# Whole weighted sum ahead of the query, attention output turned ahead of the next scores: the tile loop of a gated cross-attention and expert block

## The chip, the cores and the metric

One core of a Trainium2 chip. The time is device microseconds of one execution; the kernel before was run three times, and one further execution was profiled. All times below are microseconds (us) from the start of the profiled span unless said otherwise. PE is TensorE (PEld its weight loads), DVE is VectorE, ACT is ScalarE, POOL is GpSimd, SP is SyncE.

## The reference

```python
# x (2, 1024, 256), context (2, 77, 256), 16 heads of 16
x = x + tanh(g_xattn) * cross_attention(layernorm(x), ctx)   # scores, mask, softmax, probs @ V, @ wo.T + bo
# 8 experts, top 1
def ffn(xt):
    gates, idx = max and argmax of softmax(xt @ Wr + br)
    xn = layernorm(xt) * ln_g + ln_b
    h = relu(xn @ W1[idx] + b1[idx])
    return (h @ W2[idx] + b2[idx]) * gates
x = x + tanh(g_ffn) * ffn(layernorm(x))
```

## The kernel before, in words

The 2048 tokens are 16 tiles of 128 (`NT = 16`, `TPB = 8` a batch). The first half of the kernel is a loop `for n in range(NT)` over tiles, written out by hand for each engine; the engines meet only through semaphores, and each works through its own list in order. The second half routes the tokens, sorted by expert, through slots of 128 rows; it begins when the loop is done.

The tile loop is a pipeline. In round n, PE does the scores of tile n, `transpose_O(n-2)` (the normed attention output `On` is turned into `pA`), `transpose_P(n-1, 0)` (the first probabilities are turned into `pT`), `project(n-2)` (the turned output `OT` times `wo`, into `pB`), `transpose_P(n-1, 1)`, `transpose_x(n+1)`, `transpose_P(n-1, 2)`, the weighted sum `attend(n-1)` (probabilities times values, into `pB`, ten chunks) with its first 8 chunks, `query(n+1)`, the other 2 chunks, and `route(n)` (the router's product, moving width 8). In round 13 (`NT - 3`) PE also does `ranks(0)`, ahead of `route`; it waits for the one-hot rows `oh` of tiles 0 to 10.

DVE in round n: max and subtraction of the first half of the scores (L923, L931), with the two steps of `gate(n-4)` between them in rounds 4 to 12 (L1010, L1016); `resid(n-2)` (L957: adds `pB` to `xs`, after `project(n-2)`; `attend(n-1)` may only then write `pB`); the second half's max and subtraction; statistics (L962, L966, L891, L895); the steps of `router(n-3)`, a generator (L990, L994, L999, L1003 which makes `oh`, L1005); `normed1(n+2)` (L901, makes xh); then `norm(n-1)`, a generator of three steps (L940 waits for the weighted sum, L944, L950 makes `On`), with router steps between them; `logits` and `x_logits`. Round 3 has three steps of `mask_bias(1)`. From round 14 on, steps of a table (`table_steps`) fill in between; `rank(0)` is one of its two generators and makes 11 rows of a table (L1090).

ACT copies or activates what PE turned: `copy_OT` (L639), `copy_PT` (L629 to L633), `exp` (L621), `copy_XX` (L602), `query` (L615), and writes the z and x2 parts of the row that POOL stores to DRAM (`z_row` L657, `x2_row` L650), and `gate_exp` (L662). SP's loads of the last three experts' weights wait for counts of `x2_row`. POOL has the powers of the norms, `x + bias`, and the stores of the rows.

`pA` is shared by `transpose_O`, `transpose_x` and the first half of the query; `pB` by the weighted sum, the projection and, later, the outputs of the experts. The waits that matter here are these:

```python
def transpose_O(i):
    e.wait_ge(g["dve_On"], i + 1)
    e.wait_ge(g["act_Q"], 2 * min(i + 2, NT - 1) + 1)
def project(i):
    e.wait_ge(g["act_OT"], i + 1)
# attend, at chunk 0
    e.wait_ge(g["dve_x2"], i)
# ranks
    e.wait_ge(g["dve_oh"], hi)
```

Of the kernel before, what the change touches and what calls it, by code (L numbers as in the profile page):

```python
# [20 lines left out]
NT = T // 128  # L21
# [10 lines left out]
NC = 10  # L32
# [36 lines left out]
def flamingo(nc, x, ctx_in, mask, g_x, g_f, wq, bq, wk, bk, wv, bv, wo, bo,  # L69
# [5 lines left out]
    with ExitStack() as ctx:  # L75
# [135 lines left out]
        g = {n: sem(n) for n in EVENTS}  # L211
# [383 lines left out]
        def _(e):  # L595
# [87 lines left out]
            for n in range(NT):  # L683
                if n >= 2:
                    copy_OT(n - 2)
                if n:
                    copy_PT(n - 1, 0)
                exp(n, 0)
                if n == 0:
                    exp(0, 1)  # L690
                if n:
                    copy_PT(n - 1, 1)
                    if n + 1 < NT:
                        copy_XX(n + 1)
                    copy_PT(n - 1, 2)
                    exp(n, 1)
                if n == 1:
                    e.wait_ge(g["pe_wT"], 4)
                    e.wait_ge(g["act_tg"], 1)
                    e.activation(wT["wo"][:, :, 0:D], bank["T1"].rearrange("p (k d) -> p k d", k=2), ACT.Copy,  # L700
                                 scale=tg[:, 0:1]).then_inc(g["act_wT"], 1)
                if n + 1 < NT:
                    query(n + 1)
                if n >= 3:
                    z_row(n - 3)
                if n == 2:
                    e.wait_ge(g["dve_pois"], 1)
                if n >= 2:
                    x2_row(n - 2)
                if n >= 3:  # L710
                    gate_exp(n - 3)
                if n == 1:
                    e.wait_ge(g["pe_wT"], 5)
                    e.wait_ge(g["pe_lg"], 2)
                    e.activation(wT["wo"][:, :, D:DX], bank["T1"][:, 0:16].rearrange("p (k d) -> p k d", k=2),
                                 ACT.Copy, scale=tg[:, 0:1]).then_inc(g["act_wT"], 1)
                    e.activation(boR[:, :], bank["T1"][:, 16:24], ACT.Copy, scale=tg[:, 0:1]).then_inc(g["act_wT"], 1)
            r_of = {}

# [165 lines left out]
        def _(e):  # L885
# [351 lines left out]
            def table_steps(k):  # L1237
                for _ in range(k):
                    next(tabled, None)

            for n in range(NT):
# [5 lines left out]
                t = smax(n, 0)  # L1247
# [25 lines left out]
                if n == 3:  # L1273
                    e.wait_ge(g["dve_pois"], 1)
                    mask_bias(1)
                next(routed, None)
                next(x_stats, None)
                table_steps(3)
                next(routed, None)
                if n + 2 < NT:  # L1280
                    normed1(n + 2)
# [292 lines left out]
        def _(e):  # L1574
# [84 lines left out]

            def attend(i, chunks=range(NC)):  # L1660
                b = i // TPB
                if i == 0:
                    e.wait_ge(g["dve_VB"], 2)
                for c in chunks:
                    n = chunk_rows(c)
# [3 lines left out]
                    if c == 0 and i:  # L1669
                        e.wait_ge(g["dve_x2"], i)  # L1670
                    t = e.matmul(pB[:, 17 * h0:17 * h0 + 51], PT[i % 2][0:n, c, :], VB[0:n, b, c, :], start=(c == 0),  # L1671
                                 stop=(c == NC - 1), skip_group_check=True)
                if c == NC - 1:
                    t.then_inc(g["pe_PV"], 1)

# [84 lines left out]
            for n in range(NT):  # L1760
                scores(n)
                if n >= 2:
                    transpose_O(n - 2)
                    transpose_P(n - 1, 0)
                    project(n - 2)
# [30 lines left out]
                if n:  # L1796
# [7 lines left out]
                    transpose_P(n - 1, 2)  # L1804
                    attend(n - 1, range(8 if n > 1 else NC))
                if n == 1:
                    e.wait_ge(g["act_PT"], 2)
                    weight("wo", "T1")
                if n + 1 < NT:
                    if n >= 1:  # L1810
                        e.wait_ge(g["act_PT"], 3 * n)
                    query(n + 1)
                if n > 1:
                    attend(n - 1, range(8, NC))
                if n == 0:
# [23 lines left out]
                if n:  # L1839
                    route(n)  # L1840

            def first_ids():
# [268 lines left out]
```

## Time and profile before

| what | value |
|---|---|
| median of 3 runs | 278.11 us (276.93 to 278.54) |
| profiled execution | 278.49 us, its span 276.7 us |
| PE busy | 268.3 us, 97% of the span |
| PEld busy | 238.7 us, 86% |
| DVE busy | 201.5 us, 73% |
| ACT busy | 166.3 us, 60% |
| POOL busy | 131.9 us, 48% |
| chain that ended last | PE 80%, DVE 8%, issue 6% |
| mean granted TensorE clock | 0.991 |

Busy time says how long an engine had something to do. The end of a matmul is modelled, so a PE that is reported busy can still have waited a little; the weight loads (PEld) show idle time more plainly, and the time from one group of instructions to the next shows what a round really costs.

### The profile page before, as it was taken

The page shows a single profiled execution, that of the slowest core. Times are in us where ns is not written, and L with a number is a line of the kernel's source. Part 1 is how long each engine was busy: PE and PEld are TensorE (multiplying, and loading weights), DVE is VectorE, ACT ScalarE, POOL GpSimd, SP SyncE. Part 2 cuts the span into 40 slices and gives each one's busy share as a digit, 9 for nine tenths or more (in the row PEclk, how much of TensorE's full clock was granted, in tenths as well). Part 3 has the DMA queues.
Part 4 walks back from the last instruction along what each step waited for, and adds up shares of the span by engine and source line. Part 5 has one row for each costly group of instructions (what it writes and reads, how often), then busy time and mean ns, then how long its engine had stood idle before and what let it go on. Part 6 is the DMA issues. An engine that isn't in the chain of part 4 may idle for free.

```text
span 276.7 us, 7230 instructions
## 1 busy us (share of the span) xinstructions
PE 268.3 (97%) x2310; PEld 238.7 (86%) x2310; DVE 201.5 (73%) x687; ACT 166.3 (60%) x444; POOL 131.9 (48%) x255
## 2 busy tenths in 40 slices
PE   8999999999999999999999999999999999999993
PEld 4879899999899999988899799899878799988992
DVE  6699479888888888899679966985547545543564
ACT  2435467777677777676776655795438445453551
POOL 3444146677877778644775424432322042222421
PEclk9999799999999999999999999999999999999998
DMA  7999998010112464565343131412201122120222
GB/s 213 257 307 374 372 376 286 5 38 39 41 40 52 191 191 186 189 195 190 116 118 118 48 104 48 129 50 80 60 23 46 49 63 61 61 57 27 59 60 61
DMA packets 19948, 34.42 MB, mean 124 GB/s; under 512 B 2392, under 2 KB 14486, under 8 KB 19899
## 3 DMA queue, kind: packets, MB, share of 16 engines
q1 hardware_dynamic: 15945, 22.33, 24.8%
q0 software_dynamic: 3808, 11.42, 13.3%
q8 instruction: 25, 0.41, 0.6%
q14 instruction: 24, 0.20, 0.2%
q10 hardware_dynamic: 146, 0.07, 0.1%
HBM read 27.45 MB, written 6.75 MB: 124 GB/s over the span
## 4 chain that ended last, share of the span: by engine, by line
PE 80%; DVE 8%; issue 6%; POOL 3%; DMA 2%; DVEq 0%; POOLq 0%
PE pS L1897 17%; PE pB L1671 12%; PE pB L1967 9%; PE pT L1582 7%; PE pB L1689 7%; PE pA L1582 5%; PE pB L1972 4%; PE pS L1625 4%; PE pA L1605 3%; PE pT L1605 2%; PE pT L1699 2%; POOL out_dram L473 1%; POOL zin L456 1%; DMA W2s<-in_ctx_dram 1%; DVE hA L1346 1%
## 5 line engine op out<-in xcount | busy, mean ns | idle before, releaser
L1897 PE MATMUL pS<-znf,W1c 128*128 128x128 f32 x576 | 71.0, 276 | 0.3 <-DVE ticks L1334 0.3
L1897 PEld LDWEIGHTS pS<-znf,W1c 128*128 128x128 f32 x576 | 67.2, 192 | 3.0 <-issue 2.9
L473 POOL DMA_INDIRECT out_dram<-yo,idxs x17 | 17.2, 1010 | 76.4 <-DVE yo L1377 72.4
L1967 PE MATMUL pB<-W2p,hT 128*128 128x512 f32 x136 | 38.9, 408 | 0.5 <-DVE ticks L1386 0.4
L761 ACT ACTIVATE hA<-pS,b1s 128x128 f32<-128x128 f32 x72 | 20.5, 367 | 30.5 <-PE pS L1897 24.9
L1346 DVE TENSOR_SCALAR hA<-pS,b1s 128x128 f32<-128x128 f32 x72 | 20.2, 344 | 20.3 <-PE pS L1897 19.9
L621 ACT ACTIVATE Pb<-Pb 128x616 f32<-128x616 f32 x32 | 23.0, 718 | 15.4 <-DVE Pb L931 15.4
L772 ACT ACTIVATE hT<-hA 128x512 fp32r<-128x512 f32 x36 | 22.9, 640 | 14.5 <-DVE hA L1346 14.5
L1967 PEld LDWEIGHTS pB<-W2p,hT 128*128 128x128 f32 x136 | 23.0, 188 | 5.9 <-issue 2.1
L923 DVE TENSOR_REDUCE mx<-pS 128x8 f32<-128x616 f32 x32 | 25.3, 789 | 1.8 <-PE pS L1629 1.8
L456 POOL DMA_INDIRECT zin<-rows_dram,idxg x21 | 22.1, 1051 | 9.5 <-issue 5.3
L931 DVE TENSOR_TENSOR Pb<-pS,mx 128x616 f32<-128x616 f32 x32 | 25.3, 792 | 0.8
L1582 PE MATMUL pT<-cst,Pb 128*128 128x128 f32 (+1 forms) x160 | 25.5, 277 | 0.0
L1353 DVE TENSOR_TENSOR hT<-hA,hT 128x512 fp32r<-128x512 f32 x36 | 24.3, 687 | 1.4 <-ACT hT L772 0.2
L1972 PEld LDWEIGHTS pB<-W2p,hT 128*128 128x128 f32 x136 | 20.7, 188 | 3.3 <-DVE hT L1353 0.3
L1972 PE MATMUL pB<-W2p,hT 128*128 128x256 f32 x136 | 21.6, 280 | 0.0
L1582 PEld LDWEIGHTS pT<-cst,Pb 128*128 128x128 f32 (+1 forms) x160 | 19.5, 142 | 2.1 <-issue 0.2
L1689 PE MATMUL pB<-woT,OT 128*128 128x264 f32 x64 | 19.2, 425 | 0.5
L1671 PE MATMUL pB<-VB,PT 128*128 128x51 f32 (+1 forms) x160 | 19.5, 270 | 0.0
L1671 PE MATMUL pB<-VB,PT_xh 128*128 128x51 f32 (+1 forms) x160 | 19.4, 270 | 0.0
L1671 PEld LDWEIGHTS pB<-VB,PT 128*128 128x128 f32 (+1 forms) x160 | 19.0, 192 | 0.3 <-issue 0.2
L1671 PEld LDWEIGHTS pB<-VB,PT_xh 128*128 128x128 f32 (+1 forms) x160 | 19.0, 192 | 0.3 <-issue 0.3
(282 smaller groups left out, 546.6 us busy)
## 6 DMA issues: line engine op xcount, KB each, us to landing
W1s<-in_L_ffn_W_dram SPq DMA_DIRECT2D x8, 1024.0 KB, 10.8
W2s<-in_L_ffn_W_dram SPq DMA_DIRECT2D x8, 1024.0 KB, 11.4
rows_dram<-pay POOLq DMA_DIRECT2D x12, 260.0 KB, 3.9
xs<-in_x_dram SPq DMA_DIRECT2D x3, 512.0 KB, 8.6
rows_dram<-pay SPq DMA_DIRECT2D x4, 260.0 KB, 2.0
W2s<-in_sel_dram SPq DMA_DIRECT2D x1, 385.0 KB
zin<-rows_dram,idxg POOLq DMA_INDIRECT x21, 3.7
out_dram<-yo,idxs POOLq DMA_INDIRECT x17
```

The source lines that it names most:

```text
L456: e.indirect_dma_start(zin[s % NZ][:, :], None, scratch[0:128 * GA, :] if s < KA else scratch, bass.IndirectOffsetOnAxis(ap=idxg[:, s:s + ...
L621: e.activation(p2, p2, ACT.Exp, scale=0.25).then_inc(g["act_P"], 1)
L923: e.tensor_reduce(mx[:, i % 2, 8 * m:8 * m + 8].rearrange("p (n h) -> p n h", n=2), heads(m), AX.X, ALU.max).then_inc(g["dve_own"], 1)
L931: e.tensor_tensor(Pb[i % 2][:, 616 * m:616 * m + 616].rearrange("p (n h k) -> p n h k", n=2, h=4), heads(m), mx[:, i % 2, 8 * m:8 * m + 8] ...
L1346: e.tensor_scalar(half_of(s, 1)[:, 128 * c:128 * c + 128], pS[:, 2 * (s % 2) + 1, 128 * c:128 * c + 128], b1s[:, 4 + c, s:s + 1], 0.0, ALU ...
L1353: e.tensor_tensor(lo, half_of(s, n)[:, :], hi, ALU.subtract).then_inc(g["dve_hT"], 1)
L1582: return e.transpose(o, i, ident[0:n, 0:n])
L1671: t = e.matmul(pB[:, 17 * h0:17 * h0 + 51], PT[i % 2][0:n, c, :], VB[0:n, b, c, :], start=(c == 0), stop=(c == NC - 1), skip_group_check=True)
L1689: t = e.matmul(pB[:, 0:DX], OT[:, k, :], wT["wo"][:, k, :], start=(k == 0), stop=(k == 1))
L1897: t = e.matmul(pS[:, 2 * (s % 2) + n, 128 * c:128 * c + 128], W1c[k][n][:, 128 * c:128 * c + 128], znf[s % 2][:, 128 * k:128 * k + 128], s ...
L1967: e.matmul(o2, hT[s % 2][0][:, 128 * c:128 * c + 128], W2p[c // 2][:, :, D * (c % 2):D * (c % 2) + D], start=False, stop=True, skip_group_ ...
L1972: t = e.matmul(o, hT[s % 2][1][:, 128 * c:128 * c + 128], W2p[c // 2][:, 0, D * (c % 2):D * (c % 2) + D], start=False, stop=True, skip_gro ...
```

## The change

It moves work within the tile rounds; no instruction is added or dropped. PE does all ten chunks of `attend(n-1)` ahead of `query(n+1)`, and turns the output of tile n-1 at the end of round n (rounds 1 to 14) where it turned that of tile n-2 behind the scores. ACT copies the turned output behind the query's copies, and the z row is written ahead of the second `exp`. DVE takes the three steps of the norm earlier (not in round 15): the first ahead of the aggregate of the x statistics, the others between the router's first steps; `normed1` and the rest of the router's steps come behind it.

```diff
--- before.py
+++ after.py
@@ -681,8 +681,6 @@
             copy_XX(1)
             a_steps = Count()
             for n in range(NT):
-                if n >= 2:
-                    copy_OT(n - 2)
                 if n:
                     copy_PT(n - 1, 0)
                 exp(n, 0)
@@ -693,6 +691,8 @@
                     if n + 1 < NT:
                         copy_XX(n + 1)
                     copy_PT(n - 1, 2)
+                    if n >= 3:
+                        z_row(n - 3)
                     exp(n, 1)
                 if n == 1:
                     e.wait_ge(g["pe_wT"], 4)
@@ -701,8 +701,8 @@
                                  scale=tg[:, 0:1]).then_inc(g["act_wT"], 1)
                 if n + 1 < NT:
                     query(n + 1)
-                if n >= 3:
-                    z_row(n - 3)
+                if 2 <= n < NT - 1:
+                    copy_OT(n - 1)
                 if n == 2:
                     e.wait_ge(g["dve_pois"], 1)
                 if n >= 2:
@@ -715,6 +715,7 @@
                     e.activation(wT["wo"][:, :, D:DX], bank["T1"][:, 0:16].rearrange("p (k d) -> p k d", k=2),
                                  ACT.Copy, scale=tg[:, 0:1]).then_inc(g["act_wT"], 1)
                     e.activation(boR[:, :], bank["T1"][:, 16:24], ACT.Copy, scale=tg[:, 0:1]).then_inc(g["act_wT"], 1)
+                    copy_OT(0)
             r_of = {}
 
             def regs(s):
@@ -1274,9 +1275,15 @@
                     e.wait_ge(g["dve_pois"], 1)
                     mask_bias(1)
                 next(routed, None)
+                if n < NT - 1:
+                    next(normal, None)
                 next(x_stats, None)
+                if n < NT - 1:
+                    next(normal, None)
                 table_steps(3)
                 next(routed, None)
+                if n < NT - 1:
+                    next(normal, None)
                 if n + 2 < NT:
                     normed1(n + 2)
                 table_steps(3)
@@ -1657,11 +1664,11 @@
                                   Pb[i % 2][:, 128 * c:128 * c + n])
                 t.then_inc(g["pe_PT"], 1)
 
-            def attend(i, chunks=range(NC)):
+            def attend(i):
                 b = i // TPB
                 if i == 0:
                     e.wait_ge(g["dve_VB"], 2)
-                for c in chunks:
+                for c in range(NC):
                     n = chunk_rows(c)
                     h0 = chunk_head(c)
                     if c % 4 == 0:
@@ -1670,8 +1677,7 @@
                         e.wait_ge(g["dve_x2"], i)
                     t = e.matmul(pB[:, 17 * h0:17 * h0 + 51], PT[i % 2][0:n, c, :], VB[0:n, b, c, :], start=(c == 0),
                                  stop=(c == NC - 1), skip_group_check=True)
-                if c == NC - 1:
-                    t.then_inc(g["pe_PV"], 1)
+                t.then_inc(g["pe_PV"], 1)
 
             def transpose_O(i):
                 e.wait_ge(g["dve_On"], i + 1)
@@ -1760,7 +1766,6 @@
             for n in range(NT):
                 scores(n)
                 if n >= 2:
-                    transpose_O(n - 2)
                     transpose_P(n - 1, 0)
                     project(n - 2)
                 if n == 1:
@@ -1802,7 +1807,7 @@
                     if n + 1 < NT:
                         transpose_x(n + 1)
                     transpose_P(n - 1, 2)
-                    attend(n - 1, range(8 if n > 1 else NC))
+                    attend(n - 1)
                 if n == 1:
                     e.wait_ge(g["act_PT"], 2)
                     weight("wo", "T1")
@@ -1810,8 +1815,6 @@
                     if n >= 1:
                         e.wait_ge(g["act_PT"], 3 * n)
                     query(n + 1)
-                if n > 1:
-                    attend(n - 1, range(8, NC))
                 if n == 0:
                     e.wait_ge(d["ln"], 48)
                     e.wait_ge(g["dve_V"], 2)
@@ -1838,6 +1841,8 @@
                     ranks(0)
                 if n:
                     route(n)
+                if 1 <= n < NT - 1:
+                    transpose_O(n - 1)
 
             def first_ids():
```

## Rows read from the trace of the kernel before

**Rows 1.** Stretches, score matmuls: stretch, us, busy (count), clock, DMA share, GB/s

```profile
28.99:37.40 8.41, 1.00 (x17) 0.80 1.07 380
...
87.55:94.65 7.10, 0.81 (x16) 1.00 0.55 186
...
108.84:116.55 7.71, 0.81 (x16) 1.00 0.53 173
```

**Rows 2.** Groups of lines, PEld, 44.49 to 108.84

```profile
L1689 PEld LDWEIGHTS pB<-woT,OT 128*128 128x128 f32 x36 | 6.1, 189 | 3.1 <-ACT OT L639 2.5
```

**Rows 3.** Timeline, PEld and PE, tile 10: start, us, engine, line, what

```profile
88.30 0.20 PEld L1582 LDWEIGHTS pA<-cst,On 128*128 128x128 f32 x2 [0.17 <-DVE On L950]
...
89.22 0.74 PEld L1689 LDWEIGHTS pB<-woT,OT 128*128 128x128 f32 x4 [0.28 <-ACT OT L639]
89.22 1.16 PE L1689 MATMUL pB<-woT,OT 128*128 128x264 f32 x4
...
90.98 1.86 PEld L1671 LDWEIGHTS pB<-VB,PT 128*128 128x128 f32 x16
92.76 0.53 PEld L1605 LDWEIGHTS pA<-XX,wqT 128*128 128x128 f32 x4
...
94.10 0.53 PEld L1699 LDWEIGHTS pT<-wrc,XX 128*128 128x128 f32 x4
```

**Rows 4.** Timeline, DVE, tile 10

```profile
88.46 0.78 DVE L923 TENSOR_REDUCE mx<-pS 128x8 f32<-128x616 f32 x1
89.17 0.15 DVE L1010 RECIPROCAL Lg<-Lg 128x1 f32<-128x1 f32 x1
...
90.07 0.20 DVE L1016 TENSOR_SCALAR pay<-Lg,tg 128x1 f32<-128x1 f32 x1
90.41 0.43 DVE L957 TENSOR_TENSOR xs<-pB,xs 128x264 f32<-128x264 f32 x1
...
94.35 0.17 DVE L940 TENSOR_SCALAR rden<-pB 128x16 f32<-128x16 f32 x1 [0.65 <-PE pB L1671]
...
94.92 0.43 DVE L950 TENSOR_TENSOR On<-pB,rden 128x256 f32<-128x256 f32 x1
```

**Rows 5.** Timeline, all engines, tile 8

```profile
73.61 0.72 PE L1629 MATMUL pS<-bias,identb 128*128 128x308 bf16 x4
...
74.37 0.80 DVE L923 TENSOR_REDUCE mx<-pS 128x8 f32<-128x616 f32 x1 [0.52 <-PE pS L1629]
```

**Rows 6.** Timeline, DVE and PEld, tile 13

```profile
114.19 0.41 DVE L901 TENSOR_SCALAR PT_xh<-xs,mv 128x256 f32<-128x256 f32 x1
114.51 0.15 DVE L999 TENSOR_REDUCE em<-Lg 128x1 f32<-128x8 f32 x1
114.70 0.23 DVE L1003 TENSOR_SCALAR oh<-cst,em 128x8 bf16<-128x8 f32 x1
...
115.33 0.44 PEld L1708 LDWEIGHTS pT<-oh,onesb 128*128 128x128 bf16 x11
...
116.01 0.52 PEld L1699 LDWEIGHTS pT<-wrc,XX 128*128 128x128 f32 x4
```

**Rows 7.** Timeline, DVE, tiles 14 and 15

```profile
117.44 0.79 DVE L923 TENSOR_REDUCE mx<-pS 128x8 f32<-128x616 f32 x1
...
119.49 0.43 DVE L957 TENSOR_TENSOR xs<-pB,xs 128x264 f32<-128x264 f32 x1
...
121.95 0.13 DVE L990 TENSOR_REDUCE Lg<-Lg 128x1 f32<-128x8 f32 x1
...
124.73 0.79 DVE L923 TENSOR_REDUCE mx<-pS 128x8 f32<-128x616 f32 x1
```

**Rows 8.** Timeline, PE, and a stretch with its granted clock (after POOL's count)

```profile
26.66 1.06 PE L1828 MATMUL pT<-wrc,W1s 128*128 128x8 f32 x8
...
30.00:31.00 1.00, 1.00 (x5) 1.00 (x6) 0.90 (x3) 0.35 (x1) 0.00 (x0) 0.50 1.08 401
```

**Rows 9.** Stretch of all engines: clock, DMA share and GB/s stand last

```profile
130.00:131.00 1.00, 0.99 (x16) 0.48 (x15) 0.95 (x8) 0.60 (x2) 0.90 (x3) 1.00 0.00 0
```

## The prediction

> **What bounds the kernel now.** I read the page first: PE is busy for 97% of the span and 80% of the chain that ended last. The stretches of the tile stage, taken on the score matmuls alone, give the rhythm: a tile of the loop costs 7.10 us from scores to scores, tile 2 costs 8.41 and tile 13 costs 7.71 [rows 1]. I call the start of a tile's scores S and give all times in a tile from S. Then the weight loads of nine tiles: the wait for `OT` (the copy of the turned output) ahead of `project` is 2.5 us in all, 0.28 a tile [rows 2]. The timeline of tile 10 (S = 87.55) places it: turning O starts at 0.75, `project` loads at 1.67 after 0.28 of idling, the weighted sum (`attend`) loads at 3.43, its first 16 records take 1.78 (0.111 each, so 0.22 for one turned output of two records), the query's load follows, and the last product starts at 6.55 with 0.55 until the next scores, 0.10 more than its four records need [rows 3]. The 0.17 of idling ahead of turning O is not a loss: in tile 8, where bias matmuls follow the scores, these too start 0.74 after S (72.87) and wait for nobody [rows 5].
>
> VectorE (DVE) is the second row to read. In tile 10 the max of the scores starts at 0.91, the second gate step at 2.52, the residual at 2.86, the moment `project` ends (1.67 + 1.16 = 2.83), and it ends at 3.29. `attend` may not write `pB` before that. DVE then idles 0.65 before the norm, which starts at 6.80 and has `On` ready 1.00 later [rows 3, 4].
>
> **What goes and what is added.** No instruction is added or dropped; turning O, the norm, the copy of O and the z row move.
>
> Part 1, the wait for `OT`. O of tile n-1 is now turned behind the last product of tile n, and the copy (0.15 to 0.55 after the next S, estimated from 0.38 us of copy) is done before `project` wants it at 1.17 (1.67 less 0.28 of wait, less 0.22 of turning). PE alone would then reach `attend` at 2.93 (3.43 - 0.28 - 0.22). If nothing else bound it, a tile would save the whole 0.28.
>
> Part 2, what is late next: the residual. The max starts at 0.85, because scores end at 0.81 and DVE, no longer carrying the norm there, follows PE by 0.04, as it does in tile 8 [rows 5]. From the max to the second gate step is 1.61 [rows 4]. The step itself lasts 0.20 and I give it 0.13, as DVE starts its next instruction some 0.07 before the end of the last. The residual starts at 0.85 + 1.61 + 0.13 = 2.59, ends at 3.02, and `attend` loads at 3.08. That is 0.35 earlier than 3.43, not 0.50. The 0.22 of turning O comes back at the end of the tile: 0.35 - 0.22 = 0.13, and I take 0.12. Bounds: 0.28 if `attend` doesn't wait for the residual, -0.07 if DVE doesn't overlap. The row decides between these: the max lasts 0.78 and the next starts 0.71 behind it [rows 4]. The Trainium skill, "VectorE: DVE Perf Modes", section "The DRAIN you can't avoid", says that the next instruction doesn't start until the pipe is empty. Read as full durations with no overlap, it would put the residual about 0.2 later and turn each tile's gain into that loss; the trace does not agree with that reading, by 0.07 us an instruction.
>
> Part 3, does turning O wait itself? `attend` loads at 3.08, 20 records take 2.22, the norm starts 0.25 behind the end (94.35 against 94.10 in tile 10; so 5.55), `On` is ready at 6.54. PE gets there at 5.30 + 0.90 (8 records of the query) + 0.45 (4 of the last product) = 6.65. Slack 0.1, so no wait, but no more than that. S of the next tile is 6.65 + 0.22 + 0.10 = 6.97. The query's copies on ScalarE are ready at the same moment within 0.05. The z row on ScalarE (0.5) fills the 0.58 of idling ahead of the second exp and costs nothing if that cover holds; if it doesn't, the query's copy still has 0.5 of slack. The copy of O goes ahead of the x row, which triggers the last weight loads; that delays them by some 0.4 to 0.9, and the DMA engines are already empty at 130.0, well before the routed stage needs the weights [rows 9].
>
> Tiles 4 to 7 and 9 to 12: 8 x 0.12 = 1.0 saved. Tile 8: the scores end 0.5 later and DVE is late by as much, so `attend` comes only 0.19 earlier and the 0.22 of turning is not covered: 0.0. Tile 3: three more small steps of DVE sit ahead of the norm now: 0.0. The entry (tiles 1, 2): the first O is turned before the clock falls, worth about 0.2, and one more turning lies ahead of tile 3: 0.0, bounds -0.25 and +0.25.
>
> Part 4, the price, in tile 13. `ranks(0)` stands behind the query in PE's order and waits for the one-hot row `oh` of tile 10, which DVE makes in this very tile. Before, DVE finished the router's steps without waiting for `attend`: `oh` is ready at 6.09 (114.70 + 0.22 - 108.84) and PE comes for it at 6.49 [rows 6]. Now the norm's first step stands in front of them in DVE's queue and waits for the whole weighted sum. This tile has no gate steps, so I put the residual 0.13 earlier, at 2.46; `attend` loads at 2.95 and ends at 5.17. The norm starts at 5.42 and `On` at 5.98 (0.57 behind, as in tile 10 [rows 4]); the next xh starts at 6.32 (0.1 ahead of the end of `On`), the min at 6.64 (0.32 behind), `oh` at 6.83 (0.19 behind) and is ready at 7.06 [rows 6]. PE has finished the query at 5.17 + 0.90 = 6.07 and waits until 7.12: a new stall of 1.05. Then the ranks, 0.68 [rows 6], the last product 0.45, turning O 0.22 and 0.10: the next S is at 8.57, against 7.71. Lost: 0.86. Bounds 0.6 and 1.0.
>
> Part 5, tiles 14 and 15. DVE works there without a break, from the max of tile 14 at 117.44 to that of tile 15 at 124.73, 7.29 [rows 7]. The norm's wait is put into that. The residual is at 2.05 behind the max as before (DVE's own pace), so `attend` loads at 0.85 + 2.05 + 0.49 = 3.39 and ends at 5.61; the norm can start at 5.86. DVE is there at 0.85 + (121.95 - 117.44) + 0.04 = 5.40. It idles 0.46, and 0.12 more between norm steps that the router's steps filled before. All of it is added to DVE's unbroken chain, so the max of tile 15 is 0.58 later; less 0.04 for its earlier start: 0.54 lost. From there (norm of tile 14, first ids, the tail) the order is unchanged and the delay is carried. Bounds 0.3 and 0.7.
>
> **The sum.** -1.0 (eight tiles) + 0.0 (tiles 1 to 3, 8) + 0.86 + 0.54 = +0.4 us. The profiled execution took 278.49 (span 276.7 and 1.8 around it); the median of the three runs is 0.4 lower, 278.11. On that median: 278.5. What a measurement of this kernel can tell from no change is about 0.5%, 1.4 us, so I forecast no change that can be told. With the bounds of all parts (-2.2 to +0.6 for the eight tiles, 0.6 to 1.0, 0.3 to 0.7, 0.25 either way) the forecast's own range is 276.5 to 280.6.
>
> **Rivals.**
> 1. *It does what it seems to do.* `attend` doesn't wait for the residual and PE saves 0.28 in each of some twelve tiles, and `oh` comes in time: 278.1 - 3.4 = 274.7. With the losses of parts 4 and 5 on top, 12 x 0.28 - 1.4 = 2.0, 276.1. For it: PE is the bound. Against: the residual's chain is DVE's own pace and reads 3.08 against 2.93. It decides if the residual ends before 2.87. Chance 0.13 for both.
> 2. *Slower: the clock.* In tile 2 PE is at its lower level (granted 0.50, so 1.2 of 2.4 GHz, from 30.0 to 31.0), soon after it did nothing but products of width 8 from 26.66 to the scores at 28.99 [rows 8], and the tile took 8.41 - 7.10 = 1.3 us more than the rhythm [rows 1]. In tile 13 PE would now idle 1.05 and then do narrow products for 1.1: 2.2 us of the same sort. If the clock falls there, 278.5 + 1.3 = 279.8. Against: half a microsecond of dense turning and scores follows at once, and before that comes a dense query. Chance 0.13. The Trainium skill, "TensorE: Matmul & The Clock Gate", Part 1, ties the level to how busy PE has lately been; the trace agrees that it fell behind thin work, and no run yet shows what idle time here does.
> 3. *Slower: turning O waits.* Part 3 has 0.1 of slack. If the norm comes 0.25 later than I reckon (the aggregate and the router step in between cost more than the steps that stood there), turning O waits 0.15 in nine tiles, +1.4: 279.9. Chance 0.12.
>
> **How the numbers follow.** Forecast 0.62, rivals 0.13, 0.13, 0.12. The two slow rivals lie at 279.8 and 279.9, just past the 279.5 that counts as slower; with a little of the forecast's upper end, slower gets 0.22. Faster needs 276.7: rival 1 and the forecast's lowest end, 0.15. No change 0.63. The range reaches to the slow rivals and to the milder form of rival 1: 276.2 to 280.2.
>
> **What the profile after would show.** From scores to scores 6.97 in the plain tiles, about 8.6 in tile 13, 7.5 in tile 14. PE's wait ahead of `project` gone, a short one ahead of `attend` on the residual, a wait of about 1 us at the ranks' first load on `oh`. DVE idle ahead of the norm 0.35 instead of 0.65. I am wrong if plain tiles read 6.82 (rival 1), if the granted clock falls below 1 behind tile 13 (rival 2), or if loads of the turned O idle on DVE's `On` (rival 3).

## The result, and the profile after

The changed kernel took 285.24 us (median of four executions: 281.71, 283.25, 287.22 and 289.06), the kernel before 277.88 beside it. The ratio is 1.018, with an interval of 1.011 to 1.025: slower, though the interval does not tell whether by 2%. The two longest of the four count as slow executions and are left out of the ratio. The forecast was 278.5, its range 276.2 to 280.2. The profiled execution took 281.71 (span 279.9, mean clock 0.985), the quickest of the four, so its profile shows only part of the loss.

First the windows from scores to scores, for tiles 10, 13 and 14; the columns are those of [rows 1].

```profile
87.13:94.23 7.10, 0.81 (x17) 1.00 0.48 186
108.42:117.58 9.16, 0.81 (x17) 1.00 0.45 145
117.58:126.23 8.65, 1.11 (x16) 0.80 0.45 156
```

The plain tile is as long as before, 7.10, and I had said 6.97. Tile 13 is 9.16 instead of 8.57, and tile 14, forecast at 7.5, is 8.65 at a mean clock of 0.80.

When the scores of tile 1 start differs from one execution to the next (18.46 before, 17.29 after; in all profiles 17.3 to 19.0), whatever the kernel. So I count from there to the end of the span; "rest" is tile 15 and all that follows the loop:

| from scores to scores | before | after | difference |
|---|---|---|---|
| tile 1 | 10.53 | 10.81 | +0.28 |
| tiles 2, 3 | 15.50 | 15.63 | +0.13 |
| tiles 4 to 12 | 64.35 | 64.69 | +0.34 |
| tile 13 | 7.71 | 9.16 | +1.45 |
| tile 14 | 7.15 | 8.65 | +1.50 |
| rest | 153.00 | 153.67 | +0.67 |
| sum | 258.24 | 262.61 | +4.37 |

The difference of the rest is no steady loss. In the five profiles of kernels with the changed end of the loop in which the clock did not fall there (this one and those of experiments 1, 2, 5 and 9), the rest lies between 152.9 and 154.4. In tiles 4 to 12 the loss stands in tile 4 (7.29, where the residual starts 0.19 later than in tile 10) and in tile 8 (7.72 against 7.59).

Where a plain tile's time went is read in the groups of PEld over the stretch of [rows 2], and then in the timeline of tile 10 (S = 87.13), the same tile as in [rows 3, 4].

```profile
L1695 PEld LDWEIGHTS pB<-woT,OT 128*128 128x128 f32 x36 | 6.1, 190 | 0.6
L1632 PEld LDWEIGHTS pS<-Kbd,QT 32*128 32x128 f32 x145 | 5.4, 184 | 1.7 <-ACT QT L615 1.5 <-issue 0.2
```

```profile
87.13 0.58 PEld L1632 LDWEIGHTS pS<-Kbd,QT 32*128 32x128 f32 x16 [0.17 <-ACT QT L615]
...
88.25 0.75 PEld L1695 LDWEIGHTS pB<-woT,OT 128*128 128x128 f32 x4
...
90.29 2.31 PEld L1678 LDWEIGHTS pB<-VB,PT 128*128 128x128 f32 x20 [0.26 <-issue]
92.51 0.53 PEld L1612 LDWEIGHTS pA<-XX,wqT 128*128 128x128 f32 x4
...
93.81 0.25 PEld L1589 LDWEIGHTS pA<-cst,On 128*128 128x128 f32 x2
94.23 0.44 PEld L1632 LDWEIGHTS pS<-Kbd,QT 32*128 32x128 f32 x12 [0.17 <-ACT QT L615]
```

DVE, and the second copy of the query on ACT, in the same tile:

```profile
88.00 0.80 DVE L924 TENSOR_REDUCE mx<-pS 128x8 f32<-128x616 f32 x1 [0.30 <-PE pS L1632]
...
89.75 0.42 DVE L958 TENSOR_TENSOR xs<-pB,xs 128x264 f32<-128x264 f32 x1
```

```profile
93.72 0.37 ACT L615 ACTIVATE QT<-pT,bcol 128x128 f32<-128x128 f32 x1
```

The wait for `OT` is gone, and turning O at 93.81 waits for nobody. `attend` now idles 0.26, and the residual (89.75 to 90.17) ended 0.12 before it. From `attend` to the next scores it is 3.94: 2.22 to the query, 0.90 to the last product (93.41), 0.40 to turning O and 0.42 from there to the scores. The last of these holds 0.17 of idling, which the view puts down to `QT`, the query's copy. But `QT` was ready at 94.09, 0.14 earlier. The same 0.17 stands behind the turned O where `QT` had been ready for longer: for 2.3 us ahead of the scores of tile 14, and for 0.33 ahead of those of tile 15:

```profile
125.86 0.20 PEld L1589 LDWEIGHTS pA<-cst,On 128*128 128x128 f32 x2
126.23 0.58 PEld L1632 LDWEIGHTS pS<-Kbd,QT 32*128 32x128 f32 x16 [0.17 <-issue]
```

So in the changed kernel PE's own order sets the scores once `attend` has begun, and the idling belongs to the step from turning O to the scores. Behind the last product, as the loop was before, it was 0.02. The one wait of the plain tile that could be taken out is that ahead of `attend`.

Tile 13, DVE, then PEld, then POOL, answers to [rows 6]:

```profile
113.92 0.18 DVE L941 TENSOR_SCALAR rden<-pB 128x16 f32<-128x16 f32 x1 [0.72 <-PE pB L1678]
...
114.49 0.42 DVE L951 TENSOR_TENSOR On<-pB,rden 128x256 f32<-128x256 f32 x1
...
115.34 0.75 DVE L1004 TENSOR_SCALAR oh<-cst,em 128x8 bf16<-128x8 f32 x1
```

```profile
116.16 0.35 PEld L1714 LDWEIGHTS pT<-oh,onesb 128*128 128x128 bf16 x11 [1.51 <-issue]
```

```profile
115.34 0.72 POOL L405 TENSOR_TENSOR xs<-xs,bob 128x256 f32<-128x256 f32 x1
```

The norm holds the router's steps back as foreseen, and the weight loads idle 1.51 ahead of the ranks. `oh` itself takes 0.75 where it took 0.23. It starts at the same moment as an instruction of POOL over 128x256 and ends 0.03 behind it. Behind this tile the clock falls, in these windows of all engines (granted clock third from the end):

```profile
117.00:118.00 1.00, 1.00 (x18) 0.83 (x21) 0.55 (x4) 0.32 (x2) 0.70 (x2) 0.97 0.00 0
118.00:119.00 1.00, 1.00 (x14) 0.69 (x11) 0.41 (x3) 0.65 (x4) 0.00 (x0) 0.50 0.46 179
```

It is 0.50, the lower level (1.2 of 2.4 GHz), for some 3.4 us. In the tile loop of the kernel before, the only such stretch was that of tile 2 [rows 8].

Tile 15 shows a wait that I had not reckoned with. The timelines of ACT and PEld:

```profile
133.95 0.51 ACT L650 ACTIVATE pay<-xs,pois 128x256 f32<-128x256 f32 x1 [1.63 <-DMA rows_dram<-pay]
...
134.56 0.36 ACT L639 ACTIVATE OT<-pA 128x256 f32<-128x256 f32 x1
```

```profile
129.95 2.31 PEld L1678 LDWEIGHTS pB<-VB,PT_xh 128*128 128x128 f32 x20 [1.04 <-issue]
...
134.97 0.74 PEld L1695 LDWEIGHTS pB<-woT,OT 128*128 128x128 f32 x4 [0.72 <-ACT OT L639]
```

And `attend(14)` on PEld in the kernel before:

```profile
127.33 2.31 PEld L1671 LDWEIGHTS pB<-VB,PT_xh 128*128 128x128 f32 x20 [0.27 <-issue]
```

The x2 row may only overwrite its staging buffer when an earlier row's store has left it. It waits 1.63 for that, and the copy of the turned output stands behind it in ACT's queue, with `project` behind the copy. The idling of 1.04 ahead of `attend(14)` looks dearer than it is: the sum loads 3.72 behind the tile's scores, where it loaded at 3.63 before with its waits spread over three places. It costs 0.1.

### The profile page after: what moved, and what is told of

It is laid out like the page before. It is cut to its first block, busy times and chain, and to the rows that moved or that the text cites. A ratio compares the mean times of both kernels' runs of the same rounds, so it can differ in the third digit from the quotient of the medians.

```text
span 279.9 us, 7230 instructions
## 1 busy us (share of the span) xinstructions
PE 268.6 (96%) x2310; PEld 237.2 (85%) x2310; DVE 202.9 (72%) x687; ACT 164.8 (59%) x444; POOL 132.9 (47%) x255
## 4 chain that ended last, share of the span: by engine, by line
PE 73%; DVE 9%; issue 8%; DMA 4%; POOL 4%; ACT 0%; DVEq 0%; POOLq 0%; ACTq 0%
PE pS L1902 17%; PE pB L1678 11%; PE pB L1972 9%; PE pT L1589 6%; PE pB L1695 5%; PE pB L1977 4%; PE pS L1632 4%; PE pA L1589 4%; PE pA L1612 3%; PE pT L1612 2%; DMA rows_dram<-pay 2%; PE pT L1705 2%; POOL out_dram L473 1%; DVE mx L924 1%; POOL zin L456 1%
## 5 line engine op out<-in xcount | busy, mean ns | idle before, releaser
L762 ACT ACTIVATE hA<-pS,b1s 128x128 f32<-128x128 f32 x72 | 20.5, 367 | 30.7 <-PE pS L1902 27.8
L1589 PE MATMUL pT<-cst,Pb 128*128 128x128 f32 (+1 forms) x160 | 27.0, 287 | 0.0
```

Source lines behind the costliest of these rows:

```text
L1589: return e.transpose(o, i, ident[0:n, 0:n])
```

## The experiments

Ratios are against the kernel before, run on the same chip beside them (its medians there 277.8 to 278.1). An edit is to the changed kernel unless it says otherwise.

### 1. The changed kernel again

No edit. The question was what the slower executions hold.

> The changed kernel itself, nothing edited, to see how far its executions lie apart and whether the granted clock goes with them (in four runs it took 281.7, 283.3, 287.2 and 289.1 us at mean clocks 0.985, 0.975, 0.968 and 0.957; before: 276.9 to 278.5, its profile at 0.991). Theory A (a clock that falls in the tile rounds, more often in some executions): times spread over 281 to 289 again, and every longer one has a lower clock, near 0.45 us for each 0.001. Theory B (waits alone, the spread is chance): the clock stays within 0.98 to 0.99 whatever the time.

Median 283.23 (281.32 to 287.00), ratio 1.018 (1.013 to 1.024). This time the profile fell on the slowest execution (287.00). Its windows of tiles 12 and 13:

```profile
101.21:112.28 11.07, 9.89 (x67) 0.75 0.35 124
112.28:123.52 11.24, 9.91 (x89) 0.79 0.40 118
```

Tiles 1 to 11 are as in the other profile within 0.05. What starts the loss is on the timelines of ACT, DVE and PEld in tile 12:

```profile
103.56 0.51 ACT L650 ACTIVATE pay<-xs,pois 128x256 f32<-128x256 f32 x1 [1.86 <-DMA rows_dram<-pay]
...
104.29 0.16 DVE L1011 RECIPROCAL Lg<-Lg 128x1 f32<-128x1 f32 x1 [1.40 <-ACT Lg L662]
...
104.79 0.18 PEld L1589 LDWEIGHTS pT<-cst,Pb 128*128 128x128 f32 x2 [0.87 <-ACT PT L629]
105.74 0.86 PEld L1678 LDWEIGHTS pB<-VB,PT 128*128 128x128 f32 x7 [0.78 <-issue]
```

And in the view of the row stores' line:

```profile
DMA to landing us min/median/max: 2.4/2.6/7.1
```

A row store was issued at 96.33, 1.30 behind a 1 MB weight load (95.03), and landed 7.1 us later; the quickest lands after 2.4. The x2 row waits for it. The gate's exponential and the copy of the turned probabilities are queued behind it on ACT, DVE's gate step waits for the one and PE for the other. Then the clock is at 0.50 from 106.8 to 117.0. So one late store, with the clock behind it, costs 4 us in tile 12 and 2 more in tile 13. The mechanism is that of tile 15 above, at a dearer place. Behind tile 13, whose stall of 1.49 at the ranks is there as well, the clock fell once more (123.8 to 127.3), and tile 14 took 8.65.

### 2. The norm of tile 13 in its old place

```diff
-                if n < NT - 1:
+                if n < NT - 1 and n != NT - 3:
                     next(normal, None)
```
(all three)

> The changed kernel with the norm's three steps of tile 13 alone back behind the router's steps, so that the one-hot row is ready when PE comes to the ranks. Theory A1 (the wait at the ranks costs its 1 to 1.4 us and, by the idle and narrow stretch, brings the clock down once, another 1.3 to 2): the wait at the ranks is gone, tile 13 takes about 7.8 instead of 9.2, the clock stays at 1.00 behind it, and the best execution is near 278. If this stall is what all slow executions come from, the spread closes too. Theory A2 (the contiguous weighted sum, 20 loads with moving width 51, is what lets the clock fall, in any tile): tile 13 gains its stall but the executions still spread over several us with clocks of 0.96 to 0.98.

Median 280.70 over 12 executions (278.19 to 284.08), ratio 1.009 (1.006 to 1.013), half the loss. The stall at the ranks is gone, `oh` takes 0.23 again, and tile 14 takes 7.61. In the profiled execution the x2 row waited 1.06 in tile 12, the clock fell at 108.1, and tiles 12 and 13 took 8.65 and 9.75 for that.

### 3. The kernel before, with the whole weighted sum ahead of the query

```diff
-                    attend(n - 1, range(8 if n > 1 else NC))
+                    attend(n - 1, range(NC))
...
-                if n > 1:
-                    attend(n - 1, range(8, NC))
```

> The kernel before with one part of the change alone: all ten chunks of the weighted sum ahead of the query, everything else as it was. Theory A2 (the contiguous weighted sum makes the clock fall): executions spread, clocks of 0.96 to 0.98, 280 us and more. Rival A1 (the clock falls only behind the stall at the ranks): no spread, 0.99, 278 us as before, within 1 us.

Median 282.13 (279.49 to 282.65), ratio 1.014 (1.009 to 1.019): this part alone makes the kernel slower. Tile 10 in PEld's timeline (S = 89.58):

```profile
92.99 2.31 PEld L1671 LDWEIGHTS pB<-VB,PT 128*128 128x128 f32 x20
95.22 0.53 PEld L1605 LDWEIGHTS pA<-XX,wqT 128*128 128x128 f32 x4
...
96.84 0.31 PEld L1625 LDWEIGHTS pS<-Kbd,QT 32*128 32x128 f32 x8 [0.20 <-ACT QT L615]
```

```profile
96.42 0.37 ACT L615 ACTIVATE QT<-pT,bcol 128x128 f32<-128x128 f32 x1
```

The tile takes 7.26: `attend` at 3.41, 2.23 until the query, 1.62 until the scores. Here the scores do wait for the query's copy: they start 0.05 behind its end, and so do those of all tiles from 3 to 13. Before, two chunks of the sum lay between the query and the scores and covered that copy: the query loaded at 5.21 [rows 3] and the scores came 1.89 behind it [rows 1], the time that PE's own work took. The clock stayed at 1.00 in this stretch, so the thinner work of an unbroken sum is not what costs. In the profile, counted as in the table, tiles 2 to 11 take 1.85 more than before, and tile 12 takes 8.09: the x2 row waited 1.02 for a store there, though ACT's order is that of the kernel before. The rise of the median by 4.3 is therefore not the loop's alone.

### 4. Dense products ahead of the ranks

```diff
                 if n == NT - 3:
+                    e.wait_ge(g["dve_Sm"], 2 * n + 2)
+                    warm(4, pS[:, 2, :])
                     ranks(0)
```

The four added products are 128x512 and write scores' banks that are free; nothing reads their results.

> The changed kernel with four dense bf16 products of moving width 512 (0.2 us each, results unused) in front of the ranks of tile 13, inside the stall. If idleness in tile 13 is what brings the clock down there: clock 1.00 behind tile 13, and 1.3 to 2 us less than the changed kernel in the profile although PE does more. If the fall there does not depend on that: same time as the changed kernel.

Median 285.32 (281.60 to 288.67), ratio 1.018 (1.012 to 1.023). The time can't answer the question: in the profiled execution (287.27) the x2 row waited 1.75 in tile 12, and the clock was low from 108.0 to 114.8. But it was back at 1.00 well ahead of the ranks (120.58), and it stayed there behind tile 13: tile 14 took 7.61. In the profile of experiment 1, which had the same late store and an unfilled stall, it took 8.65. The question was put again with the store's wait removed (experiment 11).

### 5. The x2 row one round later

```diff
                     if n >= 3:
                         z_row(n - 3)
+                        if n == 3:
+                            e.wait_ge(g["dve_pois"], 1)
+                        x2_row(n - 3)
                     exp(n, 1)
...
                     copy_OT(n - 1)
-                if n == 2:
-                    e.wait_ge(g["dve_pois"], 1)
-                if n >= 2:
-                    x2_row(n - 2)
```
(and `x2_row(y - 1)` ahead of `z_row(y - 1)` behind the loop)

> The changed kernel with ScalarE's x2 row moved from behind the copy of the turned output to ahead of the second exp, one tile later, so that its wait for a row store finds the store landed. Theory C (the store of tile 6 or later, in flight beside a weight load, lands 5 to 7 us after its issue; ScalarE waits for it with the gate's exp and the copy of the turned probabilities behind it, DVE and PE stall, and the clock falls behind that stall): no wait on the store in the tile loop, tile 12 takes 7.1 in every profile, the clock stays at 1.00 up to tile 13, median near 281, the spread above 283 gone. The wait at the ranks stays (9.2 for tile 13). Rival (the clock falls by the thin weighted sum alone): falls around 107 stay and the spread too.

Median 281.57, and the executions lie between 281.02 and 282.58, where the changed kernel's ten lay between 281.3 and 289.1. Ratio 1.014 (1.011 to 1.017). The group of the x2 rows on ACT (from 80 to 160) shows no wait, then come the landing times in the view of the stores' line, then PE's windows of tiles 12 to 14:

```profile
L650 ACT ACTIVATE pay<-xs,pois 128x256 f32<-128x256 f32 x10 | 5.0, 504 | 0.0
```

```profile
DMA to landing us min/median/max: 2.4/2.4/4.1
```

```profile
101.70:108.80 7.10, 7.07 (x67) 1.00 0.58 180
108.80:117.95 9.15, 7.81 (x89) 1.00 0.62 224
117.95:126.60 8.65, 8.62 (x67) 0.80 0.28 85
```

So the store waits make the executions of 283 us and more in this comparison, and tiles 13 and 14 are a loss that stays without them. A spread of 3 to 4 us is there in any case: the 29 executions of the kernel before that stand beside experiments 9 to 12 lie between 276.2 and 279.8.

The edit did two things. SP's weight loads wait for counts of the x2 row, so they moved too: in the profile they are issued 3.5 to 4.0 ahead of the row store that follows, instead of 0.5 to 1.3 in the result's profile. With that distance the stores landed after 2.4 to 2.9, so there was little left to wait for.

### 6. Both repairs

Edits 2 and 5 together.

> Both repairs: the x2 row late, and the norm of tile 13 behind the router's steps. Theory C with A1: tiles 12 and 13 take 7.1 and 7.7 to 7.8, no clock fall but the one in tile 2, median 277.5 to 278.5, no change that can be told from the kernel before. Rival (falls from the thin weighted sum): still 280 and more with clocks below 0.985.

Median 280.62 (278.94 to 281.99), ratio 1.010 (1.005 to 1.014): a miss against the expectation. Tile 13 is 7.65 and tile 14 7.61, so both repairs hold; from the scores of tile 1 on this profile is still 3.1 us longer than before's. The rows that tell why lie behind the loop, at the start of the expert products (granted clock third from the end):

```profile
139.00:140.00 1.00, 0.44 (x3) 0.89 0.22 79
140.00:141.00 1.00, 1.00 (x7) 0.50 0.02 8
```

The clock falls at 139.8, behind 1.2 us of narrow products (moving width 4 to 32, from 137.8) and 0.56 of idling, and 10.8 behind the end of `attend(14)`'s wait. The rest of that execution is 1.9 longer than before's (154.94 against 153.00). Tiles 1 to 12 (0.7) and 14 (0.46) make up nearly all of the other 1.2.

### 7. The kernel before, with the x2 row one round later

The edit of 5, on the kernel before.

> The kernel before with the x2 row moved in the same way. Its own waits on the row stores (0.91 and 0.40) lay beside idle time. Theory C: 0 to 0.5 us less than before, 277.3 to 277.8, that is, no change. Rival (the row stores cost the kernel before something already): 276.5 or less.

Median 278.09 (276.58 to 279.71), ratio 1.001 (0.997 to 1.006). There the place of the x2 row makes no difference: the waits of the kernel before for a store (0.9 and 0.4, in two tiles) had nothing urgent behind them. In the profiled execution, the slowest of the four (279.71), the clock was at 0.50 from 20.5 to 23.9 as well, and tile 1 took 11.91 instead of 10.53.

### 8. The gate steps behind the residual

```diff
                 t = smax(n, 0)
-                next(gated_row, None)
                 table_steps(2)
                 ssub(n, 0, t)
-                next(gated_row, None)
                 table_steps(3)
                 if n >= 2:
                     resid(n - 2)
...
+                next(gated_row, None)
...
                 t = smax(n, 1)
+                next(gated_row, None)
                 next(row_stats, None)
                 ssub(n, 1, t)
```

> The changed kernel with DVE's two gate steps behind the residual instead of ahead of it (0.3 us less between the scores and the weighted sum in tiles 4 to 12). Theory D (a loop sets the tile: scores, DVE to the residual, the whole weighted sum, the query, its copy on ScalarE, the next scores; PE's own work does not): the plain tile falls from 7.10 to about 6.9. Rival (PE's own work or the turned output sets it): 7.10 stays. The median says little, since the stalls in tiles 12 and 13 stay.

If the residual opens the loop, starting it earlier must shorten every plain tile by as much. PEld's timeline, tile 9 (S = 81.01):

```profile
84.04 2.31 PEld L1678 LDWEIGHTS pB<-VB,PT_xh 128*128 128x128 f32 x20
86.27 0.53 PEld L1612 LDWEIGHTS pA<-XX,wqT 128*128 128x128 f32 x4
...
87.98 0.58 PEld L1632 LDWEIGHTS pS<-Kbd,QT 32*128 32x128 f32 x16 [0.17 <-ACT QT L615]
```

`attend` loads at 3.03 instead of 3.16, and the tile is 6.97 instead of 7.10. Both fell by 0.13, and from `attend` to the scores it is 3.94 as in the changed kernel. So the loop is: scores, DVE up to the residual, `attend`, PE's own order up to the next scores. The residual itself came 0.12 earlier (2.50 instead of 2.62), not the expected 0.3. Median 281.87 (279.74 to 285.47), ratio 1.012 (1.007 to 1.017): tile 13 (9.15), tile 14 (8.70) and waits for a store (0.41 and 0.67) are still there. The profiled execution is the 285.47. Its length comes from the clock: it was low in tile 1 (19.9 to 23.3, the tile took 12.18), behind tile 13, and twice in the rest (132.5 to 139.3 and 142.8 to 146.2). So a long execution need not be one with a long store wait.

### 9. All three repairs

Edits 2, 5 and 8.

> The changed kernel with three repairs: x2 row late, norm of tile 13 behind the router's steps, gate steps behind the residual. Theory (the stalls and the loop of theory D explain all that the change lost, and each repair adds up): plain tiles 6.97, tile 13 7.65, tile 14 7.6, no fall of the clock in tiles 3 to 15; against the kernel before, tiles 4 to 12 save 1.0 us, tile 3 and 14 lose 0.6 and the last tile's weighted sum still waits 1.0 for its residual: 277.5 to 279, no change. Rival (the thin stretches make the clock fall anyway): 280 and more.

Median 279.62 over 11 executions, ratio 1.003 (1.000 to 1.007). Plain tiles 6.97, tile 13 7.65, tile 14 7.61. The median lies 0.6 above the expected 277.5 to 279. Counted from the scores of tile 1 the profile is 1.5 longer than before's, nearly all of it (1.4) in the rest. I laid that on the wait of 1.04 ahead of `attend(14)`, and the next kernel leaves the end of the loop as it was; but that wait costs 0.1, as in the result's profile. The first expert load comes 0.55 later than before's, counted from the scores of tile 15, and what follows it is 0.9 longer.

### 10. The change only as far as tile 12

Experiment 9, with the norm early only in rounds below 13, and O of tile 13 turned behind the scores of tile 15 as before.

```diff
-                if n < NT - 1 and n != NT - 3:
+                if n < NT - 3:
...
-                if 1 <= n < NT - 1:
+                if 1 <= n < NT - 2:
                     transpose_O(n - 1)
```
(and `copy_OT` and `transpose_O` of tile 13 at the head of round 15)

> As the last one, but tiles 14 and 15 in the old order as well: the norms of tiles 13 and 14 late, the turned output of tile 13 behind the scores of tile 15. Theory: tile 14 back at 7.15 and the 1.0 of waiting in tile 15 back at its old 0.3, so about 1 us less than with the three repairs alone: 276.5 to 277.8, that is 0.2 to 0.4% less than before, the first version that is not slower. Rival: the gain of the tiles 4 to 12 is given back elsewhere, 278 or more.

Median 278.15 over 12 executions (276.39 to 280.11), ratio 1.000 (0.997 to 1.003): no difference from the kernel before, and the expected 0.2 to 0.4% isn't there. Counted as in the table: tiles 4 to 12 -0.75, tile 1 +0.30, tile 14 +0.18, the rest +0.43, tiles 2, 3 and 13 -0.05; together +0.1. The gain of the loop is given back at its two ends. In tile 14, which has the whole sum but not the turned O ahead of the scores, these start 0.05 behind `QT`, as in experiment 3.

### 11. Dense products ahead of the ranks, without the store waits

Experiment 5 with the edit of 4, six products instead of four.

> The x2 row late (so nothing stalls in tile 12, and the only fall of the clock is the one behind tile 13's wait at the ranks) and six dense bf16 products of width 512 (1.3 us, results unused) inside that wait of 1.5 us. If PE's idleness ahead of it is what brings the clock down: clock 1.00 behind tile 13, tile 14 takes 7.6 instead of 8.65, median about 280.5 against 281.6. If not, nothing changes, 281.6.

Tile 13 on the timelines of PE and PEld, and the windows of tiles 13 and 14:

```profile
116.32 1.46 PE L1584 MATMUL pS<-onesb 128*128 128x512 bf16 x6
...
117.78 0.34 PEld L1714 LDWEIGHTS pT<-oh,onesb 128*128 128x128 bf16 x11 [0.50 <-DVE oh L1004]
```

```profile
110.05:119.18 9.13, 9.12 (x96) 1.00 0.64 225
119.18:126.79 7.61, 7.24 (x67) 1.00 0.35 104
```

With the stall filled, tile 13 is as long as in experiment 5, but the clock stays at 1.00 in tile 14, which takes 7.61 instead of 8.65. So the fall behind tile 13 follows from PE's idling there, and costs 1.04. Over all profiles with the late `oh`, the clock fell behind tile 13 in the four with an unfilled stall (the result's, experiments 1, 5 and 8) and in neither of the two with a filled one (experiments 4 and 11). The Trainium skill, "TensorE: Matmul & The Clock Gate", Part 1, says that the level follows how busy the engine has recently been; these two runs, alike but for the filled stall, agree. The median did not follow: 283.43 (280.48 to 284.16), ratio 1.017 (1.010 to 1.023). In the profiled execution the clock fell later instead, from 133.0 to 136.4, 2.5 behind the end of `attend(14)`'s wait. That of experiment 4, the other filled one, shows the same (135.3 to 142.1). That the time is won in the end is not shown.

### 12. The kernel before, with the gate steps behind the residual

The edit of 8, on the kernel before.

> The kernel before with only the two gate steps moved behind the residual, to see that their place gains by theory D alone. Before, the residual waited for the projection and not for DVE: plain tile 7.10 as before, 278, no change. Rival (the place of the gates helps any version): plain tile 7.0, 277.

Median 279.16, ratio 1.004 (1.000 to 1.007). The plain tile is 7.13. PE sets the pace there: the residual still waits for `project` and starts at 2.89, no earlier than before (2.86), so the freed time of DVE brings nothing. In the profile the x2 row waited 0.84 in tile 12, which took 7.46.

## Why the prediction was wrong

It was wrong in direction and size: no change was forecast, with 0.22 for slower, and the time lies 5 us above the range. By its steps:

**Part 1** was right. The wait for `OT` is gone from all nine tiles.

**Part 2** was right in kind: the residual is next, not PE. It ends at 3.04 and `attend` loads at 3.16, where I had 3.02 and 3.08. The 0.06 that I put between the two had no row behind it; it is 0.12.

**Part 3** had PE's order right and a term of it too small. I put 3.89 from `attend` to the next scores: 2.22, 0.90, 0.45, 0.22 and 0.10. It is 3.94: turning O and the step from it to the scores take 0.42 and not 0.32, the last product 0.40 and not 0.45. The 0.10 was read behind the last product; behind a turned O the loads idle 0.17. The 0.08 of part 2 and this 0.05 are all that lies between 6.97 and 7.10, and they are as large as the gain of 0.12 that I forecast. Experiment 8 confirms the loop: with the residual 0.12 earlier the tile takes 6.97. So the 1.0 us of gain in eight tiles was a loss of 0.2, and tile 8, put at 0.0, lost 0.13. The sentence "the query's copies on ScalarE are ready at the same moment within 0.05" was no miss: they are ready at 6.96. But its margin is thin, and experiment 3 shows what the two chunks of the sum between query and scores [rows 3] had covered: without them, and without the turned O in their place, the copy sets the scores and the tile takes 7.26.

The step that failed outright is the sentence on the copy of O going ahead of the x row. I asked only what this does to the weight loads. The x2 row has a wait of its own, on a store in flight, and work that PE and DVE need is queued behind it; the sum has no term for it. The wait and its price are shown (experiment 1: 1.86 of waiting, 4.0 in tile 12 with the clock), and so is that the executions above 283 us go when it goes (experiment 5; in experiment 11, with the same edit and six more products, three of four lie between 283.1 and 284.2). That the place of the copy alone brings the wait is not shown: with ACT's old order the x2 row waited 1.02 in tile 12 in experiment 3 and 0.84 in experiment 12. The distance to a weight load goes with a store's landing time, as the section on the hardware says.

Turning O indeed doesn't wait, with 0.06 of slack, so rival 3 is out. The entry was put at 0.0, bounds 0.25 either way; tile 1 costs 0.28 more (10.80 to 10.83 in all but one of the profiles of kernels that turn O at the end of the tile, the one being that of experiment 8 with its low clock; 10.54 when only the sum is moved, experiment 3), and tiles 2 and 3 cost 0.13. The small credit for turning the first O ahead of the clock's fall did not appear.

**Part 4** had the mechanism right and the size wrong by one term. The norm at 5.50, `On` at 6.07, the start of `oh` at 6.92 were forecast at 5.42, 5.98 and 6.83. But `oh` took 0.75 instead of 0.23, so the tile was 9.16 and not 8.57. The slow `oh` came in all six profiles in which the norm stood ahead of it in this tile, and in none of the others. The traces hold a likely cause: in all six it starts within 0.02 of the POOL instruction that adds the bias (0.72 long) and ends 0.03 behind it. No run moved that instruction, so this is not tested.

**Part 5** was right: 7.61 in tile 14 at full clock (experiments 2, 6, 9 and 11) against a forecast of 7.5. In the changed kernel the tile took 8.65, the difference being the clock.

**Rival 2**, at 0.13, happened, but its time of 279.8 is too low as well, since it is one loss of several. In all four profiles that came to tile 13 with the late `oh` and its stall unfilled (the result's and those of experiments 1, 5 and 8) the clock fell behind tile 13, for +1.0. I argued that the dense products around the stall would hold it. They didn't.

So the common loss is tile 13 (1.45), tile 14 (1.50) and the first twelve tiles (0.75), 3.7 us, and 0.7 more in the rest of the profiled execution. The medians agree: with the store waits away the changed kernel is 1.4% slower (experiment 5, 281.57 against 278.10). What lies above that is store waits with the clock behind them in the profiles of experiments 1 and 4, and falls of the clock elsewhere in that of experiment 8; the other long executions have no profile.

**What stays open:** whether `oh` is slow because of the POOL instruction beside it; why, at the same distance to a weight load, a store lands after 7 us in one execution and after 4.8 in another; why the clock falls in tile 1 or behind tile 15 in some executions only; and whether a filled stall would have saved its 1 us in the median.

## What to carry to other kernels

A gain of a tenth of a microsecond a tile is no larger than the gaps between instructions, so each gap in the sum needs a row of its own for the pair of steps that will meet there: here 0.06 stood for 0.12, and 0.10 for 0.17. Before work is moved from behind an instruction, ask what it covered there: two chunks of the sum, 0.45 us together, hid a copy on another engine (experiment 3), and the idle time of their own engine did not show it. When a view names a releaser, compare with when that one was done. When a copy is put ahead of or behind another on an in-order engine, look at the waits of both, a transfer's too, and at everything that is queued behind them. A new stall of a microsecond on TensorE is to be priced with a fall of the clock behind it, until a run shows that there is none.

## What the runs showed of the hardware

- A stall of 1.5 us on TensorE, with the query's products ahead of it and narrow ones behind it, was followed by 3.4 us at the lower clock (117.9 to 121.4), and waits of 0.87 and 0.78 a microsecond apart by 10.2 us of it (106.8 to 117.0, experiment 1). A wait of 1.0 ahead of `attend(14)` in tile 15 was followed by a fall 2.0 to 2.5 behind its end in three profiles (experiments 4, 8 and 11) and by none so near in six (the result's and experiments 1, 2, 5, 6 and 9).
- Over all 14 profiles, the 39 stores of 260 KB that POOL issued within 2.03 behind a weight load of 1 MB by SP landed after 3.8 to 7.1 us. Of the 30 issued 3.5 to 4.6 behind one, 29 landed after 2.4 to 3.0 and one after 4.5; the other 99 landed after 2.4 to 4.4, most of them after 2.4, and one after 6.6. The Trainium skill, "DMA: Bandwidth & Descriptors", section "Issuing engines are not separate DMA queues", says that transfers started by the scalar, sync and gpsimd engines run on the same 16 DMA engines and interleave; this agrees.
- The same DVE instruction (`oh`, 128x8) took 0.23 us in one order of the kernel and 0.73 to 0.75 in another. It was slow when it started within 0.03 of a POOL instruction over 128x154 or 128x256: so did 26 small DVE instructions of the router (`oh` of tile 10 six times, `oh` of tile 0 and the one behind it ten times each), and all 26 ended 0.02 to 0.03 behind the POOL instruction, whose length (0.44 or 0.72) they took on.
- The start of the scores of tile 1 varies by 1.7 us between profiled executions (17.3 to 19.0), more than most effects here, so profiles are to be compared from there.
